# A two-directional GRU scan on Trainium2: the projection's stores to DRAM issued by ScalarE instead of SyncE

## The chip, the cores and the metric

The kernel runs on one core of one Trainium2 chip. Times are device microseconds of one execution of the whole program, inputs and output in DRAM. All arithmetic is fp32.

## The reference, cut to what matters

x is (8, 192, 128, 128). It is normalised in 32 groups of channels, projected from 192 channels to 64, scanned by a GRU in four directions, projected back to 192 channels and added to x. All four directions share the weights.

```
seq = xs.reshape(b * A, T, c) @ Wi.T + bi            # xs: rows or columns of gn(x), forward or reversed
x_gates = seq @ W_ih.T + b_ih
def step(h, xg):
    hg = h @ W_hh.T + b_hh
    r = sigmoid(xr + hr); z = sigmoid(xz + hz)
    n = tanh(xn + r * hn)
    return (1 - z) * n + z * h
out = hs @ Wo.T + bo
x + (right + down + left + up) / 4
```

## The kernel before, in words

The eight images are worked on as four pairs. One pair fills the 128 partitions, 64 for the projected channels of each image. The projection `seq` of a pair (128 partitions, 8 blocks, 128 rows, 16 columns, 8 MB) stays in SBUF, and so does `hsum`, the sum of the states over the four directions.

**The scan of a pair (loop over g)** has 128 steps t. In each step two chains c = 0 and 1 are advanced, one for rows and one for columns; each takes both directions of its axis. TensorE adds the input part (`x_part`, L832 to L838) and the state part (`h_part`, L853 to L857) in PSUM; ScalarE computes the gates r, z and n (L655, L659, L663); VectorE makes the products between them and the new state (L989, L994, L999, L1008); GpSimd makes z times the old state and adds the new one to `hsum` (L537, L545). ScalarE's six gates of a step stand in its list in the order r0, z0, r1, n0, z1, n1 (L667 to L672). Whatever else ScalarE does in a step stands behind n1.

**The next pair beside the scan.** In steps 0 to 63 its x is loaded in chunks for the statistics. From step 71 on its projection is made in 32 tiles of 512 pixels: `project_at` gives the step at which tile m begins (7 steps for 4 tiles), `project_ends` the step at which it ends. SP loads the x tile four steps ahead (`load_next_x`, L366), TensorE multiplies, and ScalarE copies the result with its bias from PSUM to a stage (`project_next`, L635 to L644). Two tiles share one of two slots of the stage. Once both are copied, the slot (512 KB) is stored to the DRAM tensor `seq_next` (`store_seq`, L374 to L379), one step after the second tile's end: `seq_out_at`, L97. These are 16 stores for each of the three pairs that have a predecessor. They fall on steps 74, 78, 81, 85 and so on to 120, 123 and 127. In steps 78, 85, 92, 99, 106, 113 and 120 ScalarE also has a copy, in the others not. Before it writes a slot again, ScalarE waits for the slot's last store (L641).

**Back into SBUF.** `seq` of the running pair is in use until the end, from the outside in. When its inner squares are no longer needed, SP fetches the next pair's part from `seq_next` (`fetch_seq`, L381 to L389, at steps 99, 115 and 123), waiting for the stores that this part needs (L387). The outermost rows and columns (`BORDER`) come last: one piece at step 125, and three pieces after step 127 (`fetch_border`, L398 to L405), which wait for all 16 stores (L403). TensorE begins the scan of the next pair when the squares and border pieces 1 and 2 are there (L877 to L879). `hsum` is saved to DRAM in the same parts behind them (L391 to L396, L407 to L412) and cleared by GpSimd.

**The pair before beside the scan.** From the second pair on, SP also loads `hsum` (L424) and x (L434) of the pair before, the output projection runs in small units, and SP stores the result (L446).

**What sets the order.** Each engine works down its own list; the list is written out by hand, by the step tables at the head of the kernel, and engines meet at semaphores. SP's list of a step is the loop in L484 to L506: `load_hsum`, `store_out`, `load_x_again`, `load_chunk`, `load_next_x`, `store_seq`, `dump_hsum`, `fetch_seq`, `fetch_border`. Each issues one to three DMAs behind its waits. All of SP's DMAs go out on one hardware queue (q1), those of ScalarE on another (q10). ScalarE issues DMAs only before the first scan (weights) and after the last (L685, L688).

Of the kernel before, what the change touches and what calls it, by code (L numbers as in the profile page):

```python
# [5 lines left out]
def gru_scan_2d_kernel(nc: bass.Bass, x, wi_t, bi, w_ih_t, w_hh_t, b_ih, b_hh, wo_t, bo,  # L6
# [23 lines left out]
    PAIRS = B // 2  # L30
# [5 lines left out]
    TILES = PX // TILE  # L36
# [25 lines left out]
    seq_next = nc.dram_tensor("seq_next", [P, NB, HH, BW], fp32).ap()  # L62
# [34 lines left out]
    seq_out_at = {t + 1: m // 2 for t, m in project_ends.items() if m % 2 == 1}  # L97
# [32 lines left out]
    with ctx:  # L130
# [3 lines left out]
        def sem(name):  # L134
            return ctx.enter_context(nc.semaphore(name))
# [47 lines left out]
        stage = work[:, at:at + 4 * TILE].rearrange("p (s b r w) -> p s b r w", s=2, b=NB, r=2 * ROWS)  # L183
# [42 lines left out]
        staged = sem("staged")  # L226
        stage_stored = [sem(f"stage_stored{i}") for i in range(2)]
# [84 lines left out]
        def eight_rows(q):  # L312
            return slice(2 * ROWS * q, 2 * ROWS * (q + 1))
# [26 lines left out]
        def unit_bias(u):  # L340
            return bo_high[:, 0:1] if u % 3 == 2 else bo_unit[:, u % 3:u % 3 + 1]
# [4 lines left out]
        def _(sp):  # L346
# [7 lines left out]
            def load_chunk(pair, n):  # L354

                k = CHUNKS * (pair - 1) + n
                if n >= SXS:
                    sp.wait_ge(sx_used, k - SXS + 1)
                elif pair == 1:
                    sp.wait_ge(x0_used, 3 * WSLOTS + XPS)  # L360
                else:
                    sp.wait_ge(xp_used, TILES * (pair - 1))
                src = x_flat[2 * pair + n % 2, :, n // 2 * CHUNK:(n // 2 + 1) * CHUNK]
                sp.dma_start(sx[:, k % SXS, :], src).then_inc(sx_loaded[k % SXS], 16)

            def load_next_x(pair, m):  # L366
                k = TILES * (pair - 1) + m
                if m < XPS:
                    sp.wait_ge(sx_used, CHUNKS * pair)
                else:  # L370
                    sp.wait_ge(xp_used, k - XPS + 1)
                load_x(xp[:, k % XPS], pair, project_tile[m], xp_loaded[k % XPS])

            def store_seq(pair, q):  # L374

                k = TILES // 2 * (pair - 1) + q
                sp.wait_ge(staged, 2 * (k + 1))
                rows = eight_rows(TILES // 2 - 1 - q)
                sp.dma_start(seq_next[:, :, rows, :], stage[:, k % 2]).then_inc(stage_stored[k % 2], 16)  # L379

            def fetch_seq(g, k):  # L381

                for c in range(2):
                    sp.wait_ge(x_z_ready[c], T * g + grown_at[k] + 1)
                stored = TILES // 2 * g + TILES // 2 - SQUARES[k] // (2 * ROWS)
                for a in range(2):
                    sp.wait_ge(stage_stored[a], 16 * ((stored + 1 - a) // 2))  # L387
                for blocks, rows in square_pieces(k):
                    sp.dma_start(seq[:, blocks, rows, :], seq_next[:, blocks, rows, :]).then_inc(seq_fetched, 16)  # L389

            def dump_hsum(g, k):  # L391
                for c in range(2):
                    sp.wait_ge(h_added[c], T * g + grown_at[k] + 1)
                for blocks, rows in square_pieces(k):
                    sp.dma_start(hsum_last[g % 2][:, blocks, rows, :], hsum[:, blocks, rows, :])\
                      .then_inc(hsum_dumped[k], 16)  # L396
# [17 lines left out]
            def load_hsum(g, q):  # L414

                k = TILES // 2 * (g - 1) + q
                if q == 0:
                    for a in range(3):
                        sp.wait_ge(hsum_dumped[a], 16 * len(square_pieces(a)) * g)
                    for i in range(4):  # L420
                        sp.wait_ge(border_dumped[i], 16 * g)
                if k >= 2:
                    sp.wait_ge(unit_ready, 6 * (k - 1))
                sp.dma_start(hs[:, k % 2], hsum_last[(g - 1) % 2][:, :, eight_rows(q), :]).then_inc(hs_loaded[k % 2], 16)  # L424

            def load_x_again(g, n):
                k = TILES * (g - 1) + n
                if k >= XFS:
                    sp.wait_ge(xf_stored[k % XFS], 32 * (k // XFS))
                i = finish_tile_of[n]  # L430
                px = slice(i * TILE, (i + 1) * TILE)
                for a in range(2):
                    src = x_px[2 * (g - 1) + a, :, px].rearrange("(k c) n -> c k n", k=3)
                    sp.dma_start(xf[image_lanes(a, n)[1], k % XFS], src).then_inc(xf_loaded[k % XFS], 16)  # L434

            def store_out(g, n):
                k = TILES * (g - 1) + n
                s = k % XFS
                sp.wait_ge(unit_added, units_by_act(g, 3 * (n + 1)))
                if units_by_dve(g, 3 * (n + 1)):  # L440
                    sp.wait_ge(unit_finished, units_by_dve(g, 3 * (n + 1)))
                i = finish_tile_of[n]
                px = slice(i * TILE, (i + 1) * TILE)
                for a in range(2):
                    dst = out_px[2 * (g - 1) + a, :, px].rearrange("(k c) n -> c k n", k=3)
                    sp.dma_start(dst, xf[image_lanes(a, n)[0], s]).then_inc(xf_stored[s], 16)  # L446
# [32 lines left out]
            for g in range(PAIRS):  # L479
                last, more = g > 0, g + 1 < PAIRS  # L480
                if more:
                    for n in range(4):
                        load_chunk(g + 1, n)
                for t in range(-2, T):  # L484
                    if last and t in hsum_back_at:
                        load_hsum(g, hsum_back_at[t])
                    if last and t in out_at:
                        store_out(g, out_at[t])
                    if last and t in x_back_at:
                        load_x_again(g, x_back_at[t])  # L490
                    if more and 0 <= t < CHUNKS - 4:
                        load_chunk(g + 1, t + 4)
                    if more and t in x_next_at:
                        load_next_x(g + 1, x_next_at[t])
                    if more and t in seq_out_at:
                        store_seq(g + 1, seq_out_at[t])
                    if more and t in dump_at:
                        dump_hsum(g, dump_at[t])
                    if more and t in fetch_at:
                        fetch_seq(g, fetch_at[t])  # L500
                    if not more and t in xe_at:
                        for i in xe_at[t]:
                            load_last(i)
                            issued.append(i)
                    if more and t == FIRST_BORDER_AT:
                        fetch_border(g, 0)  # L506
                if more:

                    for i in (1, 2, 3):
                        fetch_border(g, i)  # L510
                    for i in (1, 0, 2, 3):
                        dump_border(g, i)
# [66 lines left out]
        def _(act):  # L579
# [42 lines left out]
            def deviation(g):  # L622
                act.wait_ge(stat_dve, NSD * g + 6)
                act.activation(sm[:, 1, :], sm[:, 0, :], ACT.Sqrt).then_inc(stat_sd, 1)
                act.preload_act_table(ACT.Sigmoid)
# [9 lines left out]
            def project_next(pair, m):  # L635
# [4 lines left out]
                if m % 2 == 0 and k >= 4:  # L640
# [2 lines left out]
                act.activation(stage[:, s, :, rows_among_eight(project_tile[m]), :], ps, ACT.Identity,  # L643
                               bias=bseq[:, 0:1]).then_inc(staged, 1)  # L644

            def add_bias(g, u):

                k = TILES * (g - 1) + u // 3
                act.wait_ge(unit_ready, UNITS * (g - 1) + u + 1)
                act.activation(xf[:, k % XFS, u % 3, :], unit_ps[:, :], ACT.Identity, bias=unit_bias(u))\  # L650
                   .then_inc(unit_added, 1)
# [13 lines left out]
            def scan(g):  # L665
                for t in range(T):
                    gate_r(g, t, 0)  # L667
                    gate_z(g, t, 0)
                    gate_r(g, t, 1)
                    gate_n(g, t, 0)  # L670
                    gate_z(g, t, 1)
                    gate_n(g, t, 1)  # L672
                    if g > 0 and t in unit_at and unit_at[t] < N_ACT:
                        add_bias(g, unit_at[t])
                    if g + 1 < PAIRS and t == S_DEVIATION:
                        deviation(g + 1)
                    if g + 1 < PAIRS and t in project_ends:
                        project_next(g + 1, project_ends[t])

# [493 lines left out]
```

## Time and profile before

| what | value |
|---|---|
| median of 3 runs | 2526.6 us (2522.61 to 2531.65) |
| profiled execution | 2523.95 us, span of its trace 2522.2 us |
| TensorE busy | 2199.8 us, 87% of the span |
| VectorE busy | 2035.9 us, 81% |
| ScalarE busy | 1621.5 us, 64% |
| GpSimd busy | 1533.2 us, 61% |
| moved by DMA | 509.25 MB, mean 202 GB/s |
| queue q1 (SP) | 478.23 MB, 69.0% of the 16 engines' span |
| queue q10 (ScalarE) | 25.85 MB, 2.9% |

Matmul ends are modelled, so the busy share of TensorE is not a share of its peak. DMA-issuing instructions are not counted as busy on any engine; in the rows they stand under the queue of their engine (SPq, ACTq), with the time for which they hold that engine's sequencer. The time "to landing" is from the issue to the last semaphore increment of the transfer. The chain that ended last gives TensorE 34%, VectorE 22% and ScalarE 22% of the span.

### The profile page before, as it was taken

How to read it: one execution, taken by the hardware profiler on the slowest of the kernel's cores; microseconds unless marked ns; L12 is line 12 of the kernel's file. 1: busy time of each engine (PE TensorE's matmuls, PEld its weight loads, DVE VectorE, ACT ScalarE, POOL GpSimd, SP SyncE). 2: the span in 40 equal slices, each digit the busy share in tenths (PEclk: the TensorE clock that was granted, in tenths of full speed). 3: DMA queues.
4: the chain of work that ended last, by engine and by line, in shares of the span. 5: the costliest groups of instructions: out<-in, count | busy, mean ns of one | idle time of the engine just before them, and what ended most of it. 6: DMA issues, size and time to landing. Idle time of an engine off the chain costs nothing.

```text
span 2522.2 us, 80883 instructions
## 1 busy us (share of the span) xinstructions
PE 2199.8 (87%) x31528; PEld 1444.4 (57%) x31528; DVE 2035.9 (81%) x4883; ACT 1621.5 (64%) x3401; POOL 1533.2 (61%) x2114
## 2 busy tenths in 40 slices
PE   0679999899979999899979999899979999999995
PEld 0345555566546666566656666566656677555574
DVE  7229999777769999787879999888867777888874
ACT  0236666677758887676758788677657888666600
POOL 2016666667766666566766666667666677666610
PEclk9999999999999999999999999999999999999998
DMA  9983332347789997589999998589986655333699
GB/s 355 288 219 96 96 96 67 85 141 218 230 241 244 240 246 177 153 224 260 308 267 250 233 246 207 142 221 263 313 258 165 152 146 129 73 94 94 154 322 363
DMA packets 325723, 509.25 MB, mean 202 GB/s; under 512 B 24928, under 2 KB 140000, under 8 KB 325344
## 3 DMA queue, kind: packets, MB, share of 16 engines
q1 hardware_dynamic: 307296, 478.23, 69.0%
q10 hardware_dynamic: 18048, 25.85, 2.9%
q8 instruction: 252, 4.13, 0.7%
q14 instruction: 127, 1.04, 0.1%
HBM read 352.98 MB, written 151.01 MB: 200 GB/s over the span
## 4 chain that ended last, share of the span: by engine, by line
PE 34%; DVE 22%; ACT 22%; issue 11%; DMA 6%; POOL 3%; SPq 1%; ACTq 0%; POOLq 0%; DVEq 0%
PE bank L855 19%; DVE r L994 8%; ACT bank L663 8%; ACT r L655 7%; ACT z L659 7%; DVE h L1008 5%; DMA work<-x 4%; DVE bank L999 4%; PE bank L856 4%; PE bank L835 3%; DVE r L989 2%; PE bank L837 2%; PE bank L953 2%; POOL hsum L529 1%; DVE bn L1119 1%
## 5 line engine op out<-in xcount | busy, mean ns | idle before, releaser
L855 PE MATMUL bank<-h,wh 64*64 64x256 f32 x6144 | 1515.0, 384 | 121.2 <-DVE h L1008 120.6
L835 PE MATMUL bank<-seq,wx 64*64 64x256 f32 x6144 | 1551.3, 385 | 62.7 <-DMA seq<-seq_next 24.0
L837 PE MATMUL bank<-seq,wx 64*64 64x256 f32 x6144 | 1551.9, 385 | 0.0
L856 PE MATMUL bank<-h,wh 64*64 64x256 f32 x6144 | 1523.9, 386 | 0.3 <-issue 0.3
L537 POOL TENSOR_TENSOR v<-z,h 128x256 f32<-128x256 f32 x1024 | 746.9, 730 | 778.7 <-ACT z L659 777.6
L855 PEld LDWEIGHTS bank<-h,wh 64*64 64x64 f32 x6144 | 727.4, 132 | 483.6 <-PE bank L837 336.6
L835 PEld LDWEIGHTS bank<-seq,wx 64*64 64x64 f32 x6144 | 741.7, 132 | 355.9 <-DVE r L994 208.2
L545 POOL TENSOR_TENSOR hsum<-hsum,h 128x256 f32<-128x256 f32 x1024 | 752.0, 734 | 94.1 <-DVE h L1008 65.1
L837 PEld LDWEIGHTS bank<-seq,wx 64*64 64x64 f32 x6144 | 740.0, 132 | 16.7 <-issue 1.2
L856 PEld LDWEIGHTS bank<-h,wh 64*64 64x64 f32 x6144 | 730.3, 132 | 1.2 <-issue 0.7
L989 DVE SCALAR_TENSOR_TENSOR r<-bank,bhh,r 128x256 f32<-128x256 f32 x1024 | 491.0, 479 | 296.0 <-ACT r L655 242.3
L659 ACT ACTIVATE z<-bank,brz 128x256 f32<-128x256 f32 x1024 | 486.5, 475 | 313.0 <-PE bank L856 300.1
L655 ACT ACTIVATE r<-bank,brz 128x256 f32<-128x256 f32 x1024 | 486.6, 475 | 211.9 <-PE bank L856 200.9
L663 ACT ACTIVATE bank<-r,bih 128x256 f32<-128x256 f32 x1024 | 488.3, 477 | 85.8 <-DVE r L994 59.4
L999 DVE SCALAR_TENSOR_TENSOR bank<-z,bank 128x256 f32<-128x256 f32 x1024 | 434.2, 424 | 74.9 <-ACT bank L663 71.2
L994 DVE TENSOR_TENSOR r<-bank,r 128x256 f32<-128x256 f32 x1024 | 431.2, 421 | 17.6
L1008 DVE TENSOR_TENSOR h<-v,bank 128x256 f32<-128x256 f32 x1024 | 425.5, 416 | 22.3 <-POOL v L537 1.6
L981 DVE BATCH_NORM_STATS2 bn<-work 128x6 f32<-128x384 f32 x384 | 212.4, 553 | 4.0 <-DMA work<-x 4.0
L819 PE MATMUL bank<-work,wo_a 64*64 64x256 f32 x768 | 202.6, 381 | 1.3 <-issue 1.3
L803 PE MATMUL bank<-work,ident 64*64 64x256 f32 x756 | 203.0, 389 | 0.0
L821 PE MATMUL bank<-work,wo_b 64*64 64x256 f32 x768 | 202.2, 381 | 0.0
L801 PE MATMUL bank<-work,ident 64*64 64x256 f32 x756 | 197.5, 381 | 0.8 <-DMA work<-x 0.8
(95 smaller groups left out, 2446.6 us busy)
## 6 DMA issues: line engine op xcount, KB each, us to landing
work<-x SPq DMA_DIRECT2D x384, 384.0 KB, 6.2
out<-work SPq DMA_DIRECT2D x192, 384.0 KB, 4.7
work<-x SPq DMA_DIRECT2D x143, 512.0 KB, 7.1
work<-x SPq DMA_DIRECT2D x286, 128.0 KB, 7.1
work<-x SPq DMA_DIRECT2D x32, 768.0 KB, 6.5
seq_next<-work SPq DMA_DIRECT2D x48, 512.0 KB, 6.3
work<-hsum_last SPq DMA_DIRECT2D x48, 512.0 KB, 6.5
seq<-x SPq DMA_DIRECT2D x17, 512.0 KB, 7.6
```

The source lines that it names most:

```text
L537: pool.tensor_tensor(v[:, c, :], z[:, c, :], h[:, c, (t + 1) % 2, :], ALU.mult).then_inc(v_ready[c], 1)
L545: pool.tensor_tensor(px, px, as_pair(h[:, c, t % 2, :], c), ALU.add).then_inc(h_added[c], 1)
L655: act.activation(r[:, c, :], rx_ps[c][:, 0:N2], ACT.Sigmoid, bias=brz[:, 0:1]).then_inc(r_ready[c], 1)
L659: act.activation(z[:, c, :], z_ps[c][:, 0:N2], ACT.Sigmoid, bias=brz[:, 1:2]).then_inc(z_ready[c], 1)
L663: act.activation(hn_ps[c][:, 0:N2], r[:, c, :], ACT.Tanh, bias=bih[:, 2:3]).then_inc(n_ready[c], 1)
L835: pe.matmul(as_pair(ps[LOW, :], c), wx[HIGH, gate, :], px[HIGH], start=start, stop=False, skip_group_check=True)
L837: return pe.matmul(as_pair(ps[HIGH, :], c), wx[LOW, gate, :], px[LOW], start=start, stop=False, skip_group_check=True)
L855: pe.matmul(ps[LOW, 0:N2], wh[LOW, gate, :], state[LOW], start=start, stop=True, skip_group_check=True)
L856: return pe.matmul(ps[HIGH, 0:N2], wh[HIGH, gate, :], state[HIGH], start=start, stop=True, skip_group_check=True)
L989: dve.scalar_tensor_tensor(out=r[:, c, :], in0=hn_ps[c][:, 0:N2], scalar=bhh[:, 2:3], in1=r[:, c, :], op0=ALU.add, op1=ALU.mult).then_inc( ...
L994: dve.tensor_tensor(r[:, c, :], rx_ps[c][:, N2:2 * N2], r[:, c, :], ALU.add).then_inc(t2_ready[c], 1)
L1008: dve.tensor_tensor(h[:, c, t % 2, :], v[:, c, :], hn_ps[c][:, N2:2 * N2], ALU.subtract)\
```

## The change

`store_seq` leaves SP's list and enters ScalarE's, with the same step table `seq_out_at`. In ScalarE's list of a step it stands behind the six gates and ahead of the copy of that step, where there is one. Its wait (both tiles of the slot copied), its source, its destination and its semaphore stay the same. All 48 stores now go out on ScalarE's DMA queue.

```
@@ SP
-            def store_seq(pair, q):
-                k = TILES // 2 * (pair - 1) + q
-                sp.wait_ge(staged, 2 * (k + 1))
-                rows = eight_rows(TILES // 2 - 1 - q)
-                sp.dma_start(seq_next[:, :, rows, :], stage[:, k % 2]).then_inc(stage_stored[k % 2], 16)
...
-                    if more and t in seq_out_at:
-                        store_seq(g + 1, seq_out_at[t])
@@ ScalarE
+            def store_seq(pair, q):
+                k = TILES // 2 * (pair - 1) + q
+                act.wait_ge(staged, 2 * (k + 1))
+                rows = eight_rows(TILES // 2 - 1 - q)
+                act.dma_start(seq_next[:, :, rows, :], stage[:, k % 2]).then_inc(stage_stored[k % 2], 16)
...
                     if g + 1 < PAIRS and t == S_DEVIATION:
                         deviation(g + 1)
+                    if g + 1 < PAIRS and t in seq_out_at:
+                        store_seq(g + 1, seq_out_at[t])
                     if g + 1 < PAIRS and t in project_ends:
                         project_next(g + 1, project_ends[t])
```

## Rows read from the trace of the kernel before

**Rows 1.** The page's head.
```profile
span 2522.2 us, 80883 instructions
```

**Rows 2.** Waits of TensorE: waited for, us in total, times, longest us.
```profile
PE bank L855 <- DVE h L1008: 120.6, 450, 2.8
...
PE bank L835 <- DMA seq<-seq_next: 24.0, 3, 8.7
```

**Rows 3.** The line of the store: times, issue in ns (min/median/max), first and last start.
```profile
L379 SPq DMA_DIRECT2D seq_next<-work x48: 549/572/1552, 492.0 to 1858.2; - x48
```

**Rows 4.** Timeline of ScalarE, first end of a pair: start us, us, [idle before <-releaser].
```profile
714.70 0.67 ACT L643 ACTIVATE work<-bank,bseq 128x512 f32<-128x512 f32 x1
715.41 0.48 ACT L655 ACTIVATE r<-bank,brz 128x256 f32<-128x256 f32 x1
...
718.40 0.48 ACT L663 ACTIVATE bank<-r,bih 128x256 f32<-128x256 f32 x1 [0.35 <-DVE r L994]
727.89 0.47 ACT L655 ACTIVATE r<-bank,brz 128x256 f32<-128x256 f32 x1 [9.02 <-PE bank L856]
```

**Rows 5.** Timeline of SP, same stretch.
```profile
715.40 0.56 SPq L379 DMA_DIRECT2D seq_next<-work  x1
718.99 0.86 SPq L405 DMA_DIRECT2D seq<-seq_next  x2
```

**Rows 6.** Timeline of ScalarE, second and third end of a pair.
```profile
1292.65 0.48 ACT L663 ACTIVATE bank<-r,bih 128x256 f32<-128x256 f32 x1 [0.35 <-DVE r L994]
1303.72 0.47 ACT L655 ACTIVATE r<-bank,brz 128x256 f32<-128x256 f32 x1 [10.59 <-PE bank L856]
...
1861.21 0.48 ACT L663 ACTIVATE bank<-r,bih 128x256 f32<-128x256 f32 x1 [0.36 <-DVE r L994]
1871.62 0.47 ACT L655 ACTIVATE r<-bank,brz 128x256 f32<-128x256 f32 x1 [9.93 <-PE bank L856]
```

**Rows 7.** Timeline of SP, second and third end of a pair.
```profile
1289.65 0.55 SPq L379 DMA_DIRECT2D seq_next<-work  x1
1294.81 1.37 SPq L405 DMA_DIRECT2D seq<-seq_next  x3
...
1858.21 0.55 SPq L379 DMA_DIRECT2D seq_next<-work  x1
1863.07 1.84 SPq L405 DMA_DIRECT2D seq<-seq_next  x3
```

**Rows 8.** ScalarE's wait at L641 in step 78 of the first pair.
```profile
L641 ACTq EVENT_SEMAPHORE  x1: 17/17/17, 511.5 to 511.5; - x1
```

**Rows 9.** Timeline of ScalarE: end of step 74, end of step 78.
```profile
496.19 0.48 ACT L655 ACTIVATE r<-bank,brz 128x256 f32<-128x256 f32 x1 [0.65 <-PE bank L856]
...
511.52 0.48 ACT L663 ACTIVATE bank<-r,bih 128x256 f32<-128x256 f32 x1 [0.27 <-DVE r L994]
512.83 0.69 ACT L643 ACTIVATE work<-bank,bseq 128x512 f32<-128x512 f32 x1 [0.83 <-PE bank L778]
```

**Rows 10.** Waits of SP: us in total, times, longest us.
```profile
SPq L387 <- DMA seq_next<-work: 24.8, 4, 10.9
```

**Rows 11.** Timeline of SP, step 99 and after, second pair.
```profile
1162.28 0.57 SPq L379 DMA_DIRECT2D seq_next<-work  x1
1173.87 0.37 SPq L389 DMA_DIRECT2D seq<-seq_next  x1
```

**Rows 12.** Timeline of TensorE, step 104 of the second pair.
```profile
1188.50 0.40 PE L751 MATMUL bank<-work,wc 64*64 64x256 f32 x1 [2.75 <-issue]
```

**Rows 13.** ScalarE's stores after the last scan, L685: issue in ns (min/median/max).
```profile
L685 ACTq DMA_DIRECT2D out<-seq x17: 378/1062/1614, 2421.5 to 2517.1; - x17
L685 ACTq DMA_DIRECT2D out<-work x15: 410/667/2317, 2413.3 to 2515.0; - x15
```

**Rows 14.** Timeline of SP in the second pair, the first of two stores of the result.
```profile
1177.29 5.71 SPq L446 DMA_DIRECT2D out<-work  x1
```

**Rows 15.** Stretch of step 99, second pair: busy us by engine, clock, DMA share, GB/s.
```profile
1162.00:1168.00 6.00, 5.75 (x99) 3.77 (x94) 4.42 (x11) 4.15 (x10) 4.21 (x6) 1.00 1.02 366
```

## The prediction

> **What bounds the kernel now.** I read the page's head first: the span is 2522.2 us [rows 1], and the profiled execution took 2523.95 us. Then the waits of the whole core. Four pairs of images are scanned one after the other, 128 steps each, and inside a step the chain is closed: state, matmuls, gate r, DVE, gate n, DVE, state. TensorE waits for h 450 times, 120.6 us in all [rows 2]. That chain is not touched. The same view has one other TensorE wait that can move: three waits of 24.0 us together for the fetch of seq from seq_next [rows 2]. It occurs once between two pairs, where the next pair's projection must be back in SBUF before the scan can go on. So I went to the three ends of a pair, engine by engine in order of time.
>
> At the first of them, SP issues the last store at 715.40, in the moment when step 127 begins on ScalarE (715.41), because the copy that it waits for ended step 126 [rows 4, 5]. It lands 3.5 us later, and SP, which has waited for that landing and nothing else, issues the border fetches at 718.99 [rows 5]. Gate r of the next pair starts at 727.89 [rows 4], 8.90 us after the first fetch was issued. At the second and third end the same distances are 1303.72 - 1294.81 = 8.91 and 1871.62 - 1863.07 = 8.55 us [rows 6, 7]. The stretch is one serial chain at each of the three ends: copy, store issue, landing, fetch, TensorE. Whatever comes onto it is paid.
>
> **The change, part by part.** What moves is 48 DMA issues of 512 KB with a median of 572 ns each [rows 3], 27.5 us of issue time, from SP's list to ScalarE's, and 48 waits with them.
>
> *Taken from SP.* SP issues transfers and computes nothing. Its loads of x for the projection stand behind the stores in order, and none of the waits for x that TensorE shows in a scan is set by the 0.57 us of one issue. I cost this at nothing; it is hidden by SP's own waiting.
>
> *When ScalarE gets to the store.* In the new program the store of step t stands behind that step's six gates. The copy it waits for ended in the step before, so the new wait is over when it is reached; nothing queues up behind it. The question is when the queue reaches it. A row of before tells: the standing wait ahead of a copy (L641) has the same place, right behind the second gate n, and its condition was long true. It is recorded at 511.5, and that gate n starts at 511.52 and runs 0.48 us [rows 8, 9]. So ScalarE's queue arrives when the last gate starts, not when it ends, and the DMA issue runs beside the gate.
>
> *Issue cost inside the scan, 45 stores.* The issue takes 0.57 us from the start of the gate, so it ends some 0.1 us after the gate. In a step without a copy ScalarE then idles 0.65 us before the next gate r; in a step with a copy behind the store, ScalarE idles 0.83 us before that copy, waiting for TensorE [rows 9]. There are 24 and 21 of these steps. Cost: nothing; the cover is 1.13 and 1.31 us from the gate's start. If the issue began only at the gate's end, 0.57 would still fit. The cover is gone only where an issue takes longer than it. The stores from ScalarE at the end of the kernel, where both queues issue, have medians of 0.67 and 1.06 us by kind and a maximum of 2.32 [rows 13], and one SP issue in the second pair runs from 1177.29 for 5.71 us [rows 14], while step 102, which has a store, is on. From the trace I count six to eight stores of the second and third pair that meet such SP work. The low bound is 0. For the high bound I let eight cost 2.32 - 1.13 = 1.2 us, together 10 us. Both medians fit under 1.13, so I take 1 us.
>
> *The last store of a pair, three times.* Here the place in the list costs. SP issued at the start of step 127. ScalarE issues behind the six gates, at the start of the last gate n: 718.40 against 715.40, 1292.65 against 1289.65, and 1861.21 against 1858.21 [rows 4 to 7]: 3.00 us later each time. Nothing else of the chain has slack, since SP waits for the landing. The border fetches, the saving of hsum behind them in SP's list, the loads for the pair after that, and TensorE all move by the same amount. Three times 3.00 is 9.0 us. The landing may change: from issue to the next fetch it was 3.6, 5.2 and 4.9 us [rows 5, 7]. All three at 3.6 would give back 2.9; all three at 5.2 would add 1.9. If the issue started at the gate's end, 0.48 more would be added three times. I take 9.0, from 6 to 12.
>
> *The fetch in mid pair, three times.* SP's longest waits for the landing of a store are at L387, 24.8 us in 4 times [rows 10], above all where the fetch of the first square waits for the store of step 99. In the second pair SP stores at 1162.28, fetches at 1173.87 [rows 11], and the x tiles that stand behind that fetch come so late that TensorE stands idle before L751 for 2.75 us [rows 12]. With the change the store is issued 3 us later at these three places. If its landing follows, up to 3 us are lost at each; if it lands sooner on ScalarE's own queue, up to 2.75 us are won at the second. When the store is issued the DMA engines are full (share 1.02, 366 GB/s [rows 15]), so it lands when the traffic drains, early or late. I take 0, from -3 to +5.
>
> The trace cannot tell how two queues share the engines here. The Trainium skill, page "DMA: Bandwidth & Descriptors", section "Queues, rings and completion order", says that each DMA engine goes round the queue rows packet by packet. By that rule the store would not stand behind SP's 2 MB, and the sum would be some 3 us less.
>
> Sum: 0 + 1 + 9.0 + 0 = +10.0 us. Against the profiled execution that is 2523.95 + 10.0 = 2534.0. The median of the three runs shown, 2526.6, lies 2.65 above that execution, so I forecast 2536.6 for a median.
>
> **Rivals.**
> 1. *Part is given back.* The landings come out at 3.6 us (-2.9) and the idle time before L751 goes (-2.75): +10.0 - 5.7 = +4.3, 2530.9. For it: the first end lands the same 512 KB in 3.6 us. Against it: nothing shows that the slower landings came of SP's queue.
> 2. *ScalarE is held.* Issues on ScalarE meet SP's long ones and outlast their cover, +6 to +10 on top: 2543 to 2547. For it: the 5.71 us issue stands in the way of a store by its time [rows 14]. Against it: only a few of 48 meet one.
> 3. *ScalarE's queue runs further ahead* and ends faster. If it passed the six gates while they still wait, the last store would go out when the copy ends, as SP's did. The ends of the pairs then cost 0, and with the store off SP's list the 2.75 us before L751 go, and with them perhaps 1 to 2 us more of late x tiles: 2526.6 - 4.5 = 2522 at best. It decides from the point where the issue is 3 us earlier than I say. Against it: the wait at L641 is recorded only as gate n starts [rows 8, 9]. The Trainium skill, page "Advanced Engine Details and Errata", section "Engine Queue Depths", gives ScalarE a queue of 8 instructions. By that rule six gates could stand in it, and this rival would hold; the row speaks against it.
> 4. *It does nothing:* the last store is not what ends last. Rows 5 and 7 exclude that: the fetch follows the landing at once. This is no case of its own.
>
> **How the numbers follow.** A measurement of this kernel can tell about 0.3% from no change, 7.6 us. Forecast 0.58, rival 1 0.22, rival 2 0.15, rival 3 0.05. The forecast's own range, +6 to +15, has about 0.08 below 7.6 us. Slower by over 0.3%: 0.50 + 0.15 = 0.65. Within: 0.22 + 0.08 = 0.30. Faster: 0.05. The range reaches from just under rival 1 to the upper part of rival 2: 2529 to 2546.
>
> **What would show it.** ScalarE's 48 issues start with the second gate n of their step and last about 0.6 us. Steps of 4.11 us with a store stay at 4.11. At each end of a pair the fetch and gate r come 3 us later, so that the distance of 12.48 us from the start of step 127 to the next gate r becomes about 15.5, and TensorE's wait of 24.0 us for seq becomes about 33. I am wrong if a store starts at the beginning of its step (rival 3), if steps with a store grow (rival 2), or if the landings at the ends shrink to 3.6 us and the total stays under 7.6 us (rival 1).

## The result, and the profile after

Eight executions of the changed kernel gave a median of 2542.8 us (2538.0 to 2546.9), eight of the kernel before 2525.8 us. The ratio is 1.0069, 95% interval 1.0055 to 1.0084: slower by 17 us. The profiled execution of the changed kernel took 2546.9 us, the slowest of its eight, so its trace shows some 4 us more than the median.

ScalarE's queue, the line of the store (issue in ns, min/median/max) and ScalarE's and SyncE's timelines at the first end of a pair:

```profile
L642 ACTq DMA_DIRECT2D seq_next<-work x48: 520/521/596, 496.1 to 1883.0; - x48
```
```profile
716.40 0.48 ACT L653 ACTIVATE r<-bank,brz 128x256 f32<-128x256 f32 x1
...
719.38 0.48 ACT L661 ACTIVATE bank<-r,bih 128x256 f32<-128x256 f32 x1 [0.35 <-DVE r L994]
719.39 0.52 ACTq L642 DMA_DIRECT2D seq_next<-work  x1
731.65 0.47 ACT L653 ACTIVATE r<-bank,brz 128x256 f32<-128x256 f32 x1 [11.79 <-PE bank L856]
```
```profile
722.94 1.35 SPq L398 DMA_DIRECT2D seq<-seq_next  x3
724.40 5.53 SPq L404 DMA_DIRECT2D hsum_last<-hsum  x4
```

These answer to [rows 3 to 5]. The store starts with the last gate n of step 127, 2.99 us after the step's start, and takes 0.52 us beside the gate. The fetch follows the landing at once. From the start of step 127 to the next gate r it is 15.25 us instead of 12.48.

Waits of TensorE and of SyncE in the changed kernel (us in total, times, longest), which answer to [rows 2, 10]; L380 is the old L387, L396 the old L403:

```profile
PE bank L835 <- DMA seq<-seq_next: 30.0, 3, 10.1
...
PE bank L751 <- issue: 15.3, 8, 2.8
```
```profile
SPq L380 <- DMA seq_next<-work: 71.3, 8, 11.1
SPq L396 <- DMA seq_next<-work: 49.3, 5, 13.7
```

The first row is the forecast loss at the ends of the pairs. The second was 3.3 us in 2 times before and was not forecast: TensorE stands before the projection of an x tile. SyncE waits for landings nearly three times as long as before ahead of the mid-pair fetches (L380), and ahead of the border fetches (L396) 49.3 us instead of 13.3.

A table by stretches shows where. Each number is the distance between two starts of gate r of chain 0 in ScalarE's timeline, as the end of the first pair above. The three columns of times come from one trace for each kernel, the ratio from all its executions. In the first pair steps 104 to 106 take 13.1 us and steps 118 to 121 take 17.8 to 17.9 us in every kernel but e6 (18.5), and are left out.

| kernel | ends of pairs 1, 2, 3 (step 127) | steps 104 to 106, pairs 2, 3 | steps 118 to 121, pairs 2, 3 | ratio |
|---|---|---|---|---|
| before | 12.5, 14.1, 13.4 | 18.0, 14.5 | 18.2, 18.6 | 1 |
| before again (e8) | 11.9, 14.0, 13.4 | 16.1, 14.3 | 18.5, 18.6 | |
| changed | 15.3, 15.4, 15.3 | 18.3, 18.4 | 22.9, 24.7 | 1.0069 |
| e1 | 12.4, 13.7, 14.5 | 18.5, 19.5 | 22.2, 22.3 | 1.0034 |
| e2 | 15.3, 15.1, 15.8 | 15.8, 14.8 | 18.2, 18.6 | 1.0036 |
| e3 | 12.2, 12.5, 14.0 | 17.4, 18.7 | 18.9, 22.7 | 1.0015 |
| e4 | 15.3, 15.2, 15.5 | 17.4, 19.1 | 18.8, 18.9 | 1.0037 |
| e5 | 12.0, 12.2, 13.3 | 15.4, 14.7 | 18.7, 18.9 | 0.9995 |
| e6 | 15.5, 15.3, 15.6 | 18.5, 19.7 | 22.6, 21.6 | 1.0058 |
| e7 | 12.8, 12.3, 13.6 | 18.7, 17.8 | 22.6, 21.3 | 1.0034 |
| e9 | 11.9, 12.2, 13.8 | 17.4, 19.0 | 18.1, 18.6 | 1.0025 |
| e10 | 12.4, 12.1, 13.2 | 14.9, 16.7 | 22.0, 18.8 | 1.0012 |
| e11 | 15.4, 16.0, 16.1 | 15.9, 15.9 | 18.2, 18.6 | 1.0047 |
| e12 | 10.6, 10.7, 10.9 | 13.6, 13.6 | 18.2, 18.2 | 0.9965 |

In the first pair the 15 steps with a store of the changed kernel, without the last, sum to 0.06 us less than before. In the later pairs one step with a store has grown outside these stretches: step 85 of the third pair, by 0.85 us, where ScalarE's copy waits that much longer for TensorE. No other trace shows it.

### The profile page after: what moved, and what is told of

Read it like the earlier page. It is cut to its first block, busy times and chain, and to the rows that moved or that the text cites. A ratio compares the mean times of both kernels' runs of the same rounds, so it can differ in the third digit from the quotient of the medians.

```text
span 2545.1 us, 80883 instructions
## 1 busy us (share of the span) xinstructions
PE 2205.8 (87%) x31528; PEld 1448.1 (57%) x31528; DVE 2035.7 (80%) x4883; ACT 1619.8 (64%) x3401; POOL 1532.4 (60%) x2114
## 4 chain that ended last, share of the span: by engine, by line
PE 35%; ACT 22%; DVE 22%; issue 11%; DMA 5%; POOL 3%; SPq 1%; ACTq 0%; DVEq 0%; POOLq 0%
PE bank L855 19%; ACT bank L661 9%; DVE r L994 8%; ACT z L657 6%; ACT r L653 6%; DVE h L1008 5%; DVE bank L999 4%; DMA work<-x 4%; PE bank L856 4%; PE bank L835 4%; PE bank L953 2%; PE bank L837 2%; DVE r L989 2%; POOL hsum L520 1%; DVE bn L1119 1%
```

## The experiments

In e1 to e12 the same values are computed, stored and fetched as in the two kernels; only who issues what, and when, differs. A time such as "the fetch at +12" counts in us from the start of the step that the sentence names. Kernels with stores on both queues have one list entry each, with a table `SP_STORES` of the stores (q = 0 to 15) that SyncE keeps, in the place of the kernel before. Ratios are to the kernel before.

**e1, e2: the ends of the pairs, alone and left out.**

```
# e1: changed kernel, with
+    SP_STORES = (TILES // 2 - 1,)
# e2: the same source, with
+    SP_STORES = tuple(range(TILES // 2 - 1))
```

> The changed kernel with one store of each pair, the 16th, back on SyncE; the other 45 stay on ScalarE behind the six gates. Theory (the time is lost in two places: the last store of a pair goes out 3 us later, and the fetches of seq in mid pair wait longer for the stores of steps 99 and 113 and hold SyncE's loads of x): the ends of the pairs are as before (12.5 to 14 us from the start of step 127 to the next gate r), steps 104 to 106 and 118 to 121 of pairs 2 and 3 stay longer. About 8 to 11 us over the kernel before, ratio 1.003 to 1.004. Rival (all is lost at the ends of the pairs, the rest is scatter of one execution): ratio 1.000. Rival (the issue on ScalarE or its own queue costs in every step): ratio 1.006.

> The kernel before with only the 16th store of each pair moved to ScalarE behind the six gates. Theory: the ends of the pairs are 2.5 to 3 us longer each, all steps in mid pair as before: 7 to 9 us over the kernel before, ratio 1.003 to 1.0035. Rival (all is lost at the ends): ratio 1.0069. Rival (all is lost in mid pair): ratio 1.000.

e1 gave 1.0034 (1.0020 to 1.0049), e2 1.0036 (1.0021 to 1.0051). Together that is 1.0070, the whole change. The expectations held in the main (the third end of e1 took 14.5 us, and the second of e2 grew by 1.0 us only), and the rivals fell: neither the ends nor the mid-pair steps are the whole. The end of the first pair in e2, ScalarE's timeline:

```profile
717.57 0.48 ACT L672 ACTIVATE bank<-r,bih 128x256 f32<-128x256 f32 x1 [0.35 <-DVE r L1005]
717.57 0.59 ACTq L653 DMA_DIRECT2D seq_next<-work  x1
729.87 0.47 ACT L664 ACTIVATE r<-bank,brz 128x256 f32<-128x256 f32 x1 [11.83 <-PE bank L867]
```

**e3: the same engine and queue, another place.**

```
                     gate_r(g, t, 0)
+                    if g + 1 < PAIRS and t in seq_out_at:
+                        store_seq(g + 1, seq_out_at[t])
                     gate_z(g, t, 0)
...
-                    if g + 1 < PAIRS and t in seq_out_at:
-                        store_seq(g + 1, seq_out_at[t])
```

> The changed kernel, all 48 stores on ScalarE, but behind the first gate r of the step instead of behind the sixth gate, so that the issue begins at the start of the step, where SyncE's began. Theory (only the 3 us of place cost, neither engine nor queue): ratio 0.999 to 1.001, the ends of the pairs as before, no step longer. Rival (the issue on ScalarE costs): steps with a store grow by up to 0.5 us, ratio 1.002 to 1.009. Rival (the second queue competes with the loads of x): steps 104 to 106 and 118 to 121 of pairs 2 and 3 stay long, ratio 1.003 to 1.006.

Measured: 1.0015 (1.0000 to 1.0030). ScalarE's timeline at the first end of a pair:

```profile
713.60 0.47 ACT L653 ACTIVATE r<-bank,brz 128x256 f32<-128x256 f32 x1
725.80 0.47 ACT L653 ACTIVATE r<-bank,brz 128x256 f32<-128x256 f32 x1 [8.74 <-PE bank L856]
```

The ends are back, 12.20 us here, with all 48 stores still issued by ScalarE. So at the ends ScalarE as the issuer costs nothing; its place in the list did. But steps 104 to 106 of the third pair and 118 to 121 of the same pair stayed long (the second pair is taken up at e8). Here my theory was incomplete: place is not all.

**e4: the two stores that the fetches wait for.** `SP_STORES = (7, 11)`.

> The changed kernel with two stores of each pair back on SyncE, those of steps 99 and 113, for which the fetches of the first and second square wait; the other 42 stay on ScalarE behind the six gates, the last one too. Theory: SyncE's waits ahead of these fetches and steps 104 to 106 and 118 to 121 are as before, the ends of the pairs stay 2.5 to 3 us longer: ratio 1.003 to 1.0035. Rival (the stores lengthen those steps by their traffic, whoever waits): ratio 1.006 to 1.007.

Measured: 1.0037 (1.0020 to 1.0054). Steps 118 to 121 returned to 18.8 and 18.9 us, steps 104 to 106 did not, against the theory (17.4 and 19.1 us), though the fetch ahead of them waited for a store that SyncE issued.

**e5, e6, e7: the order between a store and the save of hsum.** At step 113 SyncE also saves a square of hsum, 1536 and 1024 KB (the 1.8 MB in e5's expectation is too low). In the kernel before, SyncE's wait for the two copies held that save back until the store was out. SyncE's timelines in pair 2, before and in the changed kernel; ScalarE issues the store at 1232.69 in the latter:

```profile
1228.21 0.57 SPq L379 DMA_DIRECT2D seq_next<-work  x1
1228.87 1.75 SPq L395 DMA_DIRECT2D hsum_last<-hsum  x2
...
1236.04 1.69 SPq L389 DMA_DIRECT2D seq<-seq_next  x2
```
```profile
1228.89 1.04 SPq L388 DMA_DIRECT2D hsum_last<-hsum  x2
...
1245.78 0.88 SPq L382 DMA_DIRECT2D seq<-seq_next  x2
```
```profile
1232.69 0.52 ACTq L642 DMA_DIRECT2D seq_next<-work  x1
```

The store now starts 3.80 us after the save instead of 0.66 us ahead of it, and lands 13.0 us after its issue instead of 6.9, so that the fetch comes 16.2 us after the start of step 113 instead of 7.8.

```
# e5: kernel before; the two calls change places
+                    if more and t in dump_at:
+                        dump_hsum(g, dump_at[t])
                     if more and t in seq_out_at:
                         store_seq(g + 1, seq_out_at[t])
-                    if more and t in dump_at:
-                        dump_hsum(g, dump_at[t])
# e6: changed kernel; e7: e3; in dump_hsum
+                if k == 1:
+                    for a in range(2):
+                        sp.wait_ge(stage_stored[a], 16 * (TILES // 4 * g + 6))
```

> The kernel before, all stores on SyncE; only at step 113 SyncE saves the second square of hsum (1.8 MB) before it stores the stage instead of after. New theory (the moved wait had held this save back until the store was out; now the save goes out 0.7 us ahead and fills the DMA engines, and the 0.5 MB store lands some 7 us later): the fetch of seq after step 113 comes at +14 to +15 us from the step's start instead of +7 to +8, steps 118 to 121 of pairs 2 and 3 grow by 1 to 5 us each, the ends of the pairs stay: ratio 1.001 to 1.003. Rival (that fetch came late because of ScalarE's place or its queue): nothing changes, ratio 1.000.

> The changed kernel with one wait more: SyncE saves the second square of hsum only when the store of step 113 has landed. Theory of order: the fetch after step 113 comes at about +8 to +9 us instead of +16, steps 118 to 121 return to 18 to 19 us; the ends of the pairs and steps 104 to 106 stay as in the changed kernel: ratio 1.004 to 1.005 instead of 1.0069. Rival (3 us of place explain these steps): they stay at 22 to 25 us, ratio 1.007.

> All stores on ScalarE behind the first gate of their step, and the save of the second square waits for the landing of the store of step 113. Theory (place and order are all there is): steps 118 to 121 as before, ends of the pairs as before or 1 us shorter; ratio 0.999 to 1.001, against 1.0015 without the wait. Rival (a second queue costs by itself): ratio stays at 1.0015 or above.

e5, SyncE's timeline in pair 2, where step 113 starts at 1227.04:

```profile
1226.35 1.05 SPq L395 DMA_DIRECT2D hsum_last<-hsum  x2
1227.45 1.29 SPq L379 DMA_DIRECT2D seq_next<-work  x1
1240.33 1.91 SPq L389 DMA_DIRECT2D seq<-seq_next  x2
```

The order alone moves the fetch from +7.8 to +13.3 us, close to the expected +14, but of the growth that I expected from it nothing came: 0.9995 (0.9980 to 1.0009), steps 118 to 121 at 18.7 and 18.9 us. The kernel has room for a fetch at +13.8 (the third pair of e5). e3 has it at +14.9 (pair 2, steps not long) and +14.8 (pair 3, long), the changed kernel at +16.2 and +15.8 (both long). e6 and e7 missed. Holding the save back moved it to about +7, so save and fetch both ran late and the x tiles behind them too: e6 1.0058 (1.0039 to 1.0078), e7 1.0034 (1.0015 to 1.0054), no better than e3, with the fetch at only +12. So the time of the fetch by itself does not decide.

What decides is when the x tiles land. The table gives, for pairs 2 and 3, the start of the load of the x tile for step 120, its landing, and the landing of the tile for step 121 (its last piece), all against the start of the step that needs the tile.

| kernel | tile 120 issued | tile 120 landed | tile 121 landed | steps 118 to 121 |
|---|---|---|---|---|
| before | -15.0, -15.7 | -3.3, -3.6 | -0.3, +0.2 | 18.2, 18.6 |
| e5: save first, stores on SyncE | -14.1, -13.6 | -1.3, -1.5 | +1.2, +1.5 | 18.7, 18.9 |
| e4: order as before, store of step 116 on ScalarE | -15.1, -15.6 | 0.0, -0.6 | +0.9, +1.1 | 18.8, 18.9 |
| e3: both, stores at the start of their step | -13.5, -13.5 | 0.0, +0.5 | +1.4, +3.6 | 18.9, 22.7 |
| changed: both, and 3 us of place | -12.2, -12.7 | +3.8, +2.7 | +2.3, +3.7 | 22.9, 24.7 |
| e10: as e3, stores of steps 102 and 116 on SyncE | -13.7, -15.2 | -0.4, -1.5 | +3.1, +1.3 | 22.0, 18.8 |
| e6: changed, save held back | -13.8, -15.9 | +3.3, +1.8 | +2.5, +2.6 | 22.6, 21.6 |

In all traces the stretch is long where one of the two tiles lands 2.6 us or more behind the start of its step, and stays within 0.8 us of before where both land by +1.5. The turned order alone uses up about 2 us of the 3.3 and 3.6 us by which tile 120 had been early; the store of step 116 on ScalarE's queue alone uses up 3.0 to 3.3. Either fits. Together, with the place, they do not.

**e8: the kernel before again.**

> The kernel before once more, for the scatter of a single trace. Steps 70 and 71, which moved between 10.3 and 14.5 us together in the traces so far without any store near them, move again; steps 104 to 106 of pairs 2 and 3 show whether 14.5 and 18 us are two states of the same program. The ends of the pairs are 12.5 to 14.5 us, steps 118 to 121 stay at 17.8 to 18.7.

One execution, 2518.4 us. Steps 70 and 71 of the three pairs took 11.3, 14.5 and 10.3 us in the first trace and 14.5, 10.3 and 10.3 here: up to 4 us of scatter in a pair without a store near. Steps 104 to 106 of pair 2 scatter too (18.0 and 16.1), those of pair 3 do not (14.5 and 14.3). The 18.0 (step 104 alone took 8.4 us) stands alone: the traces of e2, e5, e10 and e11, with the store of step 102 on SyncE, have 14.9 to 15.9 us there, and those with it on ScalarE 17.4 to 18.7. In the third pair the two groups are 14.3 to 16.7 and 17.8 to 19.7 us.

**e9, e10: a store that overtakes.** In pairs 2 and 3 SyncE is late after step 99: it has x, hsum and result tiles to move. In the kernel before, the store of step 102 (q = 8) waited in the same list, behind the x tile for step 106.

```
# e9: kernel before, but
+    SP_STORES = tuple(q for q in range(TILES // 2) if q != 8)
# e10: e3, but
+    SP_STORES = (8, 12)
```

> The kernel before with one store of each pair on ScalarE, that of step 102 (q = 8), behind the six gates. In the kernel before SyncE reaches this store only behind its late loads of x in pairs 2 and 3, some 8 to 12 us into the stretch; from ScalarE it goes out at step 102 on a queue of its own. Theory (a store that overtakes the loads of x takes DMA time from them): the x tile of step 106 lands some 1.5 us later, steps 104 to 106 grow from 14.3 to 16 us to 17.5 to 19 us in pairs 2 and 3, nothing else changes: ratio 1.001 to 1.002. Rival (only the waits ahead of the fetches count): steps 104 to 106 as before, ratio 1.000.

> All stores on ScalarE behind the first gate of their step, except the two that run beside SyncE's late loads of x, those of steps 102 and 116 (q = 8 and 12), which are back on SyncE. Theory: steps 104 to 106 as in the kernel before (14.3 to 16 us) and 118 to 121 too (18 to 19 us), although the fetch after step 113 still comes at +14 to +15 us: ratio 0.999 to 1.001 against 1.0015. Rival (the late fetch alone makes steps 118 to 121 long): these stay at up to 22 us in a pair.

SyncE's timeline of the kernel before in pair 3, where step 106 starts at 1764.49, and e9's, of SyncE and ScalarE, where it starts at 1766.50:

```profile
1755.78 0.60 SPq L350 DMA_DIRECT2D work<-x  x1
1756.42 1.12 SPq L352 DMA_DIRECT2D work<-x  x2
1757.59 0.60 SPq L379 DMA_DIRECT2D seq_next<-work  x1
```
```profile
1757.08 0.92 SPq L352 DMA_DIRECT2D work<-x  x1
1758.04 2.03 SPq L354 DMA_DIRECT2D work<-x  x2
```
```profile
1751.86 0.52 ACTq L653 DMA_DIRECT2D seq_next<-work  x1
```

The last two pieces of that x tile, before and in e9 (KB each, median us from issue to landing):

```profile
work<-x SPq DMA_DIRECT2D x2, 128.0 KB, 9.1
```
```profile
work<-x SPq DMA_DIRECT2D x2, 128.0 KB, 10.8
```

In both kernels the x tile for step 106 is issued about 9 us ahead of the step (8.7 and 9.4). Before, the store follows it; in e9 the store has gone out 5.2 us ahead of it, into a stretch in which SyncE's own traffic is late. The tile lands 3.6 us behind the start of step 106 instead of 1.7, and step 106 takes 6.0 us before and 9.6 in e9. One store per pair, moved alone, costs 1.0025 (1.0010 to 1.0040), with steps 104 to 106 at 17.4 and 19.0 us and the other stretches of the table within the scatter. This is the second loss of the change, shown by a single edit. Its size is less sure: e4 has this loss and the one at the ends, and 1.0037, where e9 and e2 add up to 1.0061. The intervals together allow that. The reverse, e10, brought steps 104 to 106 down to 14.9 and 16.7 us, and the ratio to 1.0012 (0.9998 to 1.0026), not clearly under e3's. In steps 118 to 121 its rival holds in pair 2 (22.0 us, fetch at +14.8) and fails in pair 3 (18.8 us, fetch at +13.3).

**e11: late, but from SyncE.**

```
                 sp.wait_ge(staged, 2 * (k + 1))
+                if q == TILES // 2 - 1:
+                    sp.wait_ge(n_ready[1], T * pair)
```

> The kernel before, all stores on SyncE; only the last store of a pair also waits for the last gate n of step 127, so that it goes out about 3.5 us later, from SyncE. Theory (the time of issue counts, not the engine): the ends of the pairs grow as with ScalarE's store behind six gates, to 15 to 16.5 us, ratio 1.003 to 1.004. Rival (ScalarE's engine or queue made the ends longer): as before, 12 to 14 us, ratio 1.000.

Measured: 1.0047 (1.0027 to 1.0067), ends of 15.4, 16.0 and 16.1 us, with the store 3.54 us behind the start of step 127. From SyncE a like delay costs as much. Engine and queue are out as a cause at the ends.

**e12: a version to beat both.**

```
-    fetch_at = {grown_at[k] + 4: k for k in range(3)}
+    fetch_at = {grown_at[k] + 4 + (k == 0): k for k in range(3)}
...
-                stored = TILES // 2 * (g + 1) - (i == 0)
+                stored = TILES // 2 * (g + 1) - (1, 2, 0, 0)[i]
```

> A version meant to beat both: the kernel before with its stores on SyncE; the fetch of the first square one step later in SyncE's list, behind the load of x for step 104, and the border piece 1 waiting only for the 14 stores whose rows it needs instead of all 16, so that it is under way while the last store lands. Theory: step 104 never waits, steps 104 to 106 of pairs 2 and 3 1 to 4 us shorter, the ends of the pairs 1 to 3 us shorter each: ratio 0.995 to 0.998. Rival (the x tiles come late by DMA traffic whatever the order, and the ends by the smaller pieces): ratio 1.000.

SyncE's and ScalarE's timelines at the first end of a pair, and TensorE's wait:

```profile
713.84 0.56 SPq L379 DMA_DIRECT2D seq_next<-work  x1
714.57 4.49 SPq L405 DMA_DIRECT2D seq<-seq_next  x3
```
```profile
713.86 0.48 ACT L655 ACTIVATE r<-bank,brz 128x256 f32<-128x256 f32 x1
724.48 0.47 ACT L655 ACTIVATE r<-bank,brz 128x256 f32<-128x256 f32 x1 [7.16 <-PE bank L856]
```
```profile
PE bank L835 <- DMA seq<-seq_next: 16.3, 3, 5.6
```

The first border piece is fetched 0.73 us after the store's issue instead of after its landing, the ends take 10.6 to 10.9 us, steps 104 to 106 take 13.6 us in both pairs. Median 2512.7 us against 2523.7: 0.9965 (0.9945 to 0.9985). This version is faster than both kernels, with the stores on SyncE. It has two edits at once; the table shows both stretches shorter, but their shares of the ratio were not measured apart.

## Why the prediction was right, and where not

The forecast was +10.0 us, slower, and a median of 2536.6 us; measured were +17 us and 2542.8 us, inside the range of 2529 to 2546. That it lies inside is in part luck: the forecast's own case reached to +15 us, and the rest of the range was there for rival 2, which did not occur. By its steps:

- **When ScalarE gets to the store:** right. It was to start with the second gate n; it starts 0.00 to 0.01 us after that gate in nearly every step. The nearest row of before, [rows 8], gave this to 0.02 us. Rival 3, by which ScalarE's queue runs ahead of waiting gates, is out: no store starts at the beginning of its step. The queue of 8 that the Trainium skill gives ScalarE ("Advanced Engine Details and Errata", "Engine Queue Depths") did not let the store out ahead of the six gates.
- **Issue cost inside the scan, +1 us:** nothing is seen to be lost. All 48 issues took 0.52 to 0.60 us, under the cover of 1.13 us. The one that ran beside a long issue of SyncE, as in [rows 14], took 0.52 us too. Rival 2 did not occur.
- **The last store of a pair, +9.0 us:** right in mechanism, shown by e1, e2, e3 and e11. e2 measured 0.0036 of 2524 us, 9.1 us (5 to 13). In the trace of the changed kernel the three steps grew by 2.8, 1.4 and 1.9 us, because all three stores landed in 3.5 us, as rival 1 had it for this part; the first steps of the second and fourth pair took 1.1 and 1.5 us more, against nothing in the third.
- **"Taken from SP. I cost this at nothing":** this step failed. I looked for what the store's 0.57 us of issue held up, and not for what its wait and its place held back. Two things had hung on them: the save of hsum stood behind the store at step 113, and the store of step 102 stood behind the late loads of x. Both orders turned round.
- **"The fetch in mid pair. I take 0, from -3 to +5":** mis-sized, for the same reason. e1 measures 0.0034, 8.6 us (5 to 12). I had priced only the fetch after step 99, and for it nothing was about right: it came at +6.6, +10.8 and +10.6 us instead of +5.8, +11.6 and +10.1, since its store, issued 3 us later, landed sooner (in the second pair in 7.6 us instead of 11.5). The fetch after step 113 moved by 8 us, and steps 104 to 106 got longer not by the fetch but by a store that overtook (e9). The sentence on queues that take turns packet by packet (the Trainium skill, "DMA: Bandwidth & Descriptors", "Queues, rings and completion order") led me to name a gain of 3 us. At step 99 its own queue brought the store nothing: issued at the start of the step it took 9.8 and 10.5 us to land in pairs 2 and 3 of e3, and 11.5 and 9.5 before, 9.9 and 9.4 in e8 from SyncE. What the runs show is the other side, a store on its own queue that takes time from the loads beside it: in e9 the x tile's last pieces for step 106 took 10.8 us to land instead of 9.1.

What stays open: in steps 118 to 121 the changed kernel has the turned order, 3 us of place and the store of step 116 on another queue. The first and the last alone cost nothing that the runs can tell (e5, e4); that they add up to a late x tile is read from the landings. No run has 3 us of place alone (e6 undoes the order only by holding the save until the store has landed), and e10, in which the store of step 116 is back on SyncE, is mixed (22.0 and 18.8 us). The shares of the three losses are known to no better than some 4 us each.

## What to carry to other kernels

When a DMA is moved to another engine's list, look at both lists for order, not only for issue time: what waited behind its wait will now go ahead of it, and what it waited behind will now be overtaken. Price the moved instruction by when the new queue gets to it (behind the last waiting instruction ahead of it), and ask of every transfer that is late already what traffic will now run beside it. Where an engine serves a serial chain (copy, store, landing, fetch), 3 us of place in its list count nearly in full, while the issue time of 45 further stores, under cover, cost nothing; what they cost came by order.

## What the runs showed of the hardware that was not expected

ScalarE's DMA issues took 0.52 us against 0.57 on SyncE for the same transfer, and one ran undelayed at 1180.79 while SyncE was held in its own issues, two of 7.12 us together:

```profile
1177.97 7.12 SPq L439 DMA_DIRECT2D out<-work  x2
```
```profile
1180.79 0.52 ACTq L642 DMA_DIRECT2D seq_next<-work  x1
```

Here a long issue on one engine did not slow the issue on the other. In the stores after the last scan [rows 13] issues on both queues are longer, so this is no rule. And a 512 KB store of 512-byte pieces, issued 1.1 us behind the start of a save of 2.5 MB on the same queue (e5), landed 12.8 us after its issue, against 6.9 us when it went first.
